# An attention block with softmax row sums: normalising the probabilities on GpSimd, and grouping the probability-value steps

## The chip, the cores and the metric

The kernel runs on one core of one Trainium2 chip. The metric is the device time of one execution in microseconds. Engines are named as in the profile: PE is TensorE, DVE is VectorE, ACT is ScalarE, POOL is GpSimd, SP is SyncE, whose queue issues the DMAs.

## The reference

```python
mod = (_silu(L0_c) @ L0_wmod).reshape(L0_c.shape[0], 6, 1, -1)
sa, ca, ga, sb, cb, gb = (mod[:, 0], mod[:, 1], mod[:, 2], mod[:, 3], mod[:, 4], mod[:, 5])
...
h = _layernorm(x, axis=-1) * (1 + ca) + sa
x = x + ga * _L0_attn_ref(h, ...)
h = _layernorm(x, axis=-1) * (1 + cb) + sb
x = x + gb * _L0_ffn_ref(h, ...)        # 160 experts, 8 chosen per token, and a shared one
```

and in the attention part, with 4 batches of 512 tokens of 128 values, 16 heads of 64:

```python
scores = jnp.einsum('bhqd,bhkd->bhqk', q, k) * scale + bias      # bias by relative position
attn = jax.nn.softmax(scores, axis=-1)
a = jnp.einsum('bhqk,bhkd->bhqd', attn, v)
return a.transpose(0, 2, 1, 3).reshape(B, S, N_HEAD * HEAD_DIM) @ o_w.T
```

Everything is float32. Where a plain float32 product would be too slow, values are split in a high and a low part, and three products are summed (`PASSES`).

## The kernel before

The attention stage takes the first half of the span, the experts the second; the change touches the first alone. Its unit of work is a pair of heads: 8 pairs per batch, 32 in all. A pair has 8 units (`UNITS`), each the 128 queries of one of its two heads against all 512 keys. The code is written once as `pair(b, n)` on each engine, and each engine's `pair` lists its own steps in an order written by hand; semaphores alone tie the engines together. Pairs 0 and 1 stand ahead of a loop over three batches whose body is pairs 2 to 9 (8 and 9 are the next batch's 0 and 1), and the last batch's pairs 2 to 7 stand behind it. So the turn of a batch, with the loop's jump, lies between pair 9 and the next pair 2.

A unit goes this way. `scores` (L426, two matmuls, L434 and L436) fills one of two PSUM banks. `add_bias` (L1016, one instruction of L1028 and a read of its accumulator) adds the bias on VectorE, writes `s_sb`, one of two buffers, and yields `nmax`, the negated maximum. `exponential` (L742) on ScalarE writes `prob`, one of four buffers, and the row sum into `rsum`. `transpose_probs` (L447) turns the unit over in four 128x128 transposes into one of two PSUM banks, and `copy_probs` takes it to `PT`: even units on ScalarE, odd ones on VectorE (both by the helper of L229). When all eight are there, `attend` (L455) multiplies `PT` with the values in four blocks of keys, kb 0 to 3, two heads each, and accumulates in PSUM.

The probabilities are not normalised before that product. Instead `invert_sums` (L1040) inverts the pair's eight row sums at once, `widen_sums` (L903) on GpSimd repeats them to 128x512 in `rinv_wide`, `spread_sums` (L474) transposes that on TensorE (L479) through one of the two banks that the probabilities' transposes use, `copy_sums` (L757, L762) on ScalarE brings it to `r_sb`, and VectorE's `normalise` (L1044) multiplies the attended values with it on the way to `oT`. A table, `transpose_users` (L58), counts who uses the two banks. `project_out` (L482) follows two pairs later.

Projections for later pairs run between: `project_qk` (L397) for pair n + 2 at the end of pair n; `qk_high` (ScalarE, L740) and `qk_low` (VectorE, L1013) split its result in the middle of pair n + 1; then SyncE's `stack_pair` (L280) rearranges it by DMAs, two after `qk_high` and six after `qk_low`. `project_v` (L413) for pair n + 1 stands in pair n and is copied by `copy_v` (ScalarE, L768). The next batch's input, `hcur`, is loaded when `project_v` of pair 7 is done (L320), and `project_qk` of pair 8 waits for it. At the turn of a batch VectorE also runs `gate_y`, `update_x` (L1069) and `new_statistics` (L1061).

## Time and profile before

| | |
|---|---|
| median of three runs | 1040.71 us (1038.21 to 1040.87) |
| profiled execution | 1039.4 us, span 1037.6 us |
| busy, of the span | PE 94%, DVE 74%, ACT 67%, POOL 2% |
| mean granted TensorE clock | 0.988 |

The attention stage ends near 543 us of the span. A busy share tells how long an engine had instructions in work, not what bounds: that is read from the chain of waits, followed back from the last instruction. In the rows further below, a timeline row is start, duration, engine, line and operation, and what stands in brackets is how long the engine was idle before it and who released it.

### The profile page before, as it was taken

To read this page: it belongs to the slowest core of one execution; us is meant where nothing else is said; L and a number is where in the kernel's file an instruction comes from. 1 tells how busy PE (TensorE), PEld (TensorE's weight loads), DVE (VectorE), ACT (ScalarE), POOL (GpSimd) and SP (SyncE) were. 2 spreads that over 40 slices of the span, in tenths; PEclk is the share of its full clock that TensorE was granted. 3 is DMA by queue.
4 is the path that set the end of the run, shared out by engine and by line. 5 is a ranking of instruction groups with operands and counts; after the bars stand their busy time and mean duration, and the time that the engine had idled before them with its cause. 6 is when DMAs were issued, how large, how long until landed. Compare 5 with 4: busy or idle time off the path is not lost.

```text
span 1037.6 us, 16983 instructions
## 1 busy us (share of the span) xinstructions
PE 974.3 (94%) x4720; PEld 704.8 (68%) x4720; DVE 770.4 (74%) x1356; ACT 696.6 (67%) x1200; POOL 20.0 (2%) x36
## 2 busy tenths in 40 slices
PE   4899999999999999999978699999999999999997
PEld 2565656566666666666643487888888888888886
DVE  5766656566566665666655488999999999999997
ACT  4556656566665666666645567777777777777775
POOL 0000000000000000000000000000000000000000
PEclk9999999999999999999998899999999999999999
DMA  7874353443543534534500499999999999999992
GB/s 211 270 200 107 80 140 82 103 108 80 137 106 78 122 88 115 122 82 102 122 21 1 135 219 221 220 218 220 219 217 222 219 219 219 220 218 221 219 219 66
DMA packets 71106, 160.49 MB, mean 155 GB/s; under 512 B 10272, under 2 KB 36192, under 8 KB 60944
## 3 DMA queue, kind: packets, MB, share of 16 engines
q1 hardware_dynamic: 71056, 159.97, 68.3%
q8 instruction: 14, 0.23, 0.1%
q14 instruction: 36, 0.29, 0.1%
HBM read 105.60 MB, written 2.42 MB: 104 GB/s over the span
## 4 chain that ended last, share of the span: by engine, by line
PE 86%; ACT 4%; DMA 3%; DVE 3%; issue 2%; SPq 2%; DVEq 0%; ACTq 0%
PE ps L658 41%; PE ps L466 11%; PE ps L451 9%; PE ps L434 5%; PE ps L436 5%; PE ps L408 4%; PE ps L419 2%; PE ps L487 2%; PE ps L479 2%; ACT r_sb L762 2%; DMA k_low<-qk 1%; DMA hcur<-hT 1%; SPq L298 1%; DMA comb_rows<-strips 1%; PE ps L576 1%
## 5 line engine op out<-in xcount | busy, mean ns | idle before, releaser
L747 ACT ACTIVATE prob<-s_sb,nmax 128x512 f32<-128x512 f32 x256 | 183.6, 718 | 114.1 <-DVE nmax L1028 113.5
L658 PE MATMUL ps<-hT,wT 128*128 128x512 f32 x960 | 244.6, 391 | 0.3 <-DVE wT L1191 0.3
L1210 DVE TENSOR_TENSOR PT<-v_sb,strips 128x1024 f32<-128x1024 f32 x160 | 195.8, 1224 | 43.2 <-ACT v_sb L879 29.7
L658 PEld LDWEIGHTS ps<-hT,wT 128*128 128x128 f32 x960 | 180.8, 189 | 39.1 <-ACT strips L854 1.1
L658 PE MATMUL ps<-stack,wT 128*128 128x512 f32 x640 | 198.3, 392 | 9.0 <-DVE wT L1197 9.0
L879 ACT ACTIVATE v_sb<-ps 128x1024 f32<-128x1024 f32 x160 | 164.4, 1028 | 60.1 <-PE ps L658 59.8
L229 DVE COPY PT<-ps 128x512 f32<-128x512 f32 x128 | 88.3, 690 | 145.2 <-PE ps L451 145.0
L1197 DVE TENSOR_TENSOR wT<-PT,stack 128x1024 fp32r<-128x1024 f32 x160 | 194.8, 1218 | 0.0
L871 ACT CAST stack<-PT 128x1024 fp32r<-128x1024 f32 x160 | 166.7, 1042 | 9.0 <-DVE PT L1210 9.0
L1028 DVE CUSTOM_DVE_ANT_0 s_sb<-ps,strips 128x512 f32<-128x512 f32 x256 | 166.8, 688 | 6.6 <-PE ps L436 6.5
L451 PE MATMUL ps<-ident,prob 128*128 128x128 f32 x1024 | 140.9, 275 | 12.0 <-ACT r_sb L762 8.7
L451 PEld LDWEIGHTS ps<-ident,prob 128*128 128x128 f32 x1024 | 117.4, 141 | 42.7 <-issue 18.5
L658 PEld LDWEIGHTS ps<-stack,wT 128*128 128x128 f32 x640 | 120.3, 189 | 36.0 <-DVE wT L1197 11.1
L466 PE MATMUL ps<-PT,v_sb 128*64 128x512 f32 x512 | 123.8, 603 | 4.3 <-ACT PT L229 2.8
L434 PE MATMUL ps<-stack 128*128 128x512 f32 x256 | 113.5, 443 | 3.1 <-DMA k_low<-qk 3.1
L658 PE MATMUL ps<-wT 128*128 128x512 f32 x320 | 99.1, 391 | 0.0
L229 ACT COPY PT<-ps 128x512 f32<-128x512 f32 x128 | 73.6, 575 | 10.8 <-PE ps L451 6.9
L466 PEld LDWEIGHTS ps<-PT,v_sb 128*64 128x64 f32 x512 | 33.1, 136 | 64.0 <-issue 50.7
L658 PEld LDWEIGHTS ps<-wT 128*128 128x128 f32 x320 | 60.3, 189 | 12.7
L408 PE MATMUL ps<-hcur,wT 128*128 128x512 f32 x192 | 52.8, 412 | 10.5 <-DMA hcur<-hT 4.8
L866 ACT CAST wT<-strips 128x256 fp32r<-128x256 f32 x80 | 32.4, 406 | 38.9 <-DMA strips<-in_L_ffn_w_down 38.8
L434 PEld LDWEIGHTS ps<-stack 128*128 128x128 f32 x256 | 49.1, 192 | 11.4 <-DVE nmax L1028 2.0
(108 smaller groups left out, 758.4 us busy)
## 6 DMA issues: line engine op xcount, KB each, us to landing
strips<-comb_rows SPq DMA_DIRECT2D x158, 512.0 KB, 13.2
stack<-qk SPq DMA_DIRECT2D x128, 256.0 KB, 3.8
k_low<-qk SPq DMA_DIRECT2D x64, 128.0 KB, 3.7
hT<-qk SPq DMA_DIRECT2D x64, 128.0 KB, 3.7
strips<-bias_rows SPq DMA_DIRECT2D x3, 1792.0 KB, 10.2
strips<-in_L_ffn_w_gate SPq DMA_DIRECT2D x80, 64.0 KB, 11.6
strips<-in_L_ffn_w_down SPq DMA_DIRECT2D x80, 64.0 KB, 13.6
strips<-bias_rows SPq DMA_DIRECT2D x2, 896.0 KB, 5.2
```

The source lines that it names most:

```text
L229: return copy(dst[:, :, qt * P:(qt + 1) * P], ps[:, BANK_T + number % 2, :].rearrange("p (k s) -> p k s", s=P))
L408: last = nc.tensor.matmul(ps[:, BANK_PROJ + part, :], wT[:, a, part * H * HD + hp * P:part * H * HD + (hp + 1) * P], hcur[:, m, :], start= ...
L434: nc.tensor.matmul(ps[:, BANK_S + g % 2, :], stack[:, par, head, 0, qt * P:(qt + 1) * P], stack[:, par, head, 1, :], start=True, stop=False)
L451: last = nc.tensor.transpose(ps[:, bank, kb * P:(kb + 1) * P], prob[:, u % 4, kb * P:(kb + 1) * P], ident[:, :])
L466: last = nc.tensor.matmul(ps[head * HD:(head + 1) * HD, BANK_O, :], v_sb[:, (n // 2) % 2, kb, (n % 2) * P + head * HD:(n % 2) * P + (head ...
L658: last = nc.tensor.matmul(ps[:, bank + c, :], weights(a), rows(m, c), start=start and k == 0, stop=stop and k == 2, skip_group_check=True)
L747: nc.scalar.activation(prob[:, u % 4, :], s_sb[:, u % 2, :], ACT.Exp, bias=nmax[:, u % 4:u % 4 + 1], scale=-1.0, accum_out=rsum[:, n % 2, ...
L871: nc.scalar.copy(h_high[:, k % 4, :], weighted[:, k % 4, :]).then_inc(s_hh, 1)
L879: nc.scalar.activation(silu[:, k % 2, :], ps[:, BANK_G + 2 * half:BANK_G + 2 * half + 2, :].rearrange("p c s -> p (c s)"), ACT.Silu).then_ ...
L1028: nc.vector.tensor_tensor_reduce(out=s_sb[:, u % 2, :], in0=ps[:, BANK_S + u % 2, :], in1=backwards, scale=-1.0, scalar=3.0e38, op0=ALU.ad ...
L1197: nc.vector.tensor_tensor(h_low[:, k % 4, :], weighted[:, k % 4, :], h_high[:, k % 4, :].bitcast(F32), ALU.subtract).then_inc(s_hl, 1)
L1210: nc.vector.tensor_tensor(weighted[:, k % 4, :], silu[:, k % 2, :], cb[:, r, half * HALF:(half + 1) * HALF], ALU.mult).then_inc(s_mul, 1)
```

## The change

GpSimd multiplies each unit's probabilities by its inverted row sum, in place, before they are transposed (`normalise`, eight 128x512 multiplies per pair). For that, `invert_sums` inverts two sums at a time, four times per pair. `rinv_wide`, `spread_sums`, `copy_sums`, `r_sb` and the table of bank users go, and VectorE's multiply to `oT` becomes a copy, `copy_o`. `prob` has eight buffers, one per unit, and `add_bias` writes straight into it, so `s_sb` goes; `add_bias` of a unit now waits until the same unit of the pair before has been transposed.

The hand-written orders change too. TensorE runs all four `attend` blocks together after scores 5, `project_v` ahead of scores 4, and each unit's transposes two places later in the order than before. ScalarE's `qk_high` and VectorE's `qk_low` now stand at the end of pair n, for pair n + 2. In the diff, lines of `...` mark what is left out.

```diff
-        s_sb = sb("s_sb", [P, 2, S])
-        prob = sb("prob", [P, 4, S])
-        r_sb = sb("r_sb", [P, S])
+        prob = sb("prob", [P, UNITS, S])
         oT = sb("oT", [P, 2, S])
         yT = sb("yT", [P, S])
-        nmax = sb("nmax", [P, 4])
-        rsum = sb("rsum", [P, 2, UNITS])
-        rinv = sb("rinv", [P, 2, UNITS])
-        rinv_wide = sb("rinv_wide", [P, QT, P])
+        nmax = sb("nmax", [P, UNITS])
+        rsum = sb("rsum", [P, UNITS])
+        rinv = sb("rinv", [P, UNITS])
...
+        def copied(b, g):
+            return (s_ca if g % 2 == 0 else s_cd), b * (G // 2) + (g // 2 + 1)
...
+            def transpose_probs(b, n, u):
+                g = UNITS * n + u
+                pe.wait_ge(s_prob, b * G + (g + 1))
+                if g >= 2:
+                    pe.wait_ge(*copied(b, g - 2))
...
+                    last = nc.tensor.transpose(ps[:, BANK_T + u % 2, kb * P:(kb + 1) * P],
+                                               prob[:, u, kb * P:(kb + 1) * P], ident[:, :])
...
-            def spread_sums(b, n, final):
-                pe.wait_ge(s_wide, b * HPAIRS + (n + 1))
-                bank = bank_for(b, ("R", n, 0), final)
-                for qt in range(QT):
-                    last = nc.tensor.transpose(ps[:, bank, qt * P:(qt + 1) * P], rinv_wide[:, qt, :], ident[:, :])
-                last.then_inc(s_t, 1)
...
                 if n >= 1:
-                    transpose_probs(b, n - 1, 6, final)
-                    transpose_probs(b, n - 1, 7, final)
+                    transpose_probs(b, n - 1, 4)
+                    transpose_probs(b, n - 1, 5)
                 scores(b, n, 2)
                 scores(b, n, 3)
-                if n >= 1:
-                    attend(b, n - 1, 0, final)
-                    attend(b, n - 1, 1, final)
-                    spread_sums(b, n - 1, final)
-                transpose_probs(b, n, 0, final)
-                transpose_probs(b, n, 1, final)
-                scores(b, n, 4)
-                scores(b, n, 5)
-                if n >= 1:
-                    attend(b, n - 1, 2, final)
-                    attend(b, n - 1, 3, final)
                 if n == 0:
                     project_v(b, 0)
                 if not (final and n >= HPAIRS - 1):
                     project_v(b, n + 1)
-                transpose_probs(b, n, 2, final)
-                transpose_probs(b, n, 3, final)
+                if n >= 1:
+                    transpose_probs(b, n - 1, 6)
+                    transpose_probs(b, n - 1, 7)
+                scores(b, n, 4)
+                scores(b, n, 5)
+                if n >= 1:
+                    for kb in range(QT):
+                        attend(b, n - 1, kb)
+                transpose_probs(b, n, 0)
+                transpose_probs(b, n, 1)
                 scores(b, n, 6)
                 scores(b, n, 7)
...
                 if n == HPAIRS + 1:
                     transpose_y(b)
                 if not (final and n >= HPAIRS - 2):
                     project_qk(b, n + 2)
-                transpose_probs(b, n, 4, final)
-                transpose_probs(b, n, 5, final)
+                transpose_probs(b, n, 2)
+                transpose_probs(b, n, 3)
...
+                nc.scalar.activation(prob[:, u, :], prob[:, u, :], ACT.Exp, bias=nmax[:, u:u + 1],
+                                     scale=-1.0, accum_out=rsum[:, u:u + 1]).then_inc(s_exp, 1)
...
             def pair(b, n, final=False):
+                exponential(b, n, 0)
+                exponential(b, n, 1)
+                if n == 0:
+                    qk_high(b, 1)
                 if n >= 1:
                     copy_probs(b, n - 1, 4)
-                exponential(b, n, 0)
-                exponential(b, n, 1)
+                exponential(b, n, 2)
+                exponential(b, n, 3)
+                if n == 0:
+                    copy_v(b, 0)
+                if not (final and n >= HPAIRS - 1):
+                    copy_v(b, n + 1)
                 if n >= 1:
                     copy_probs(b, n - 1, 6)
-                if not (final and n >= HPAIRS - 1):
-                    qk_high(b, n + 1)
-                exponential(b, n, 2)
-                if n >= 1:
-                    copy_sums(b, n - 1, final)
-                exponential(b, n, 3)
-                copy_probs(b, n, 0)
                 exponential(b, n, 4)
                 exponential(b, n, 5)
                 if n == 0:
-                    copy_v(b, 0)
                     first_high(2)
                     first_high(3)
-                if not (final and n >= HPAIRS - 1):
-                    copy_v(b, n + 1)
-                copy_probs(b, n, 2)
+                copy_probs(b, n, 0)
                 exponential(b, n, 6)
                 exponential(b, n, 7)
+                if not (final and n >= HPAIRS - 2):
+                    qk_high(b, n + 2)
+                copy_probs(b, n, 2)
...
-            def widen_sums(b, n):
-                pool.wait_ge(s_rinv, b * HPAIRS + (n + 1))
-                if n >= 1:
-                    number, _, _ = tables[False][1]["R", n - 1, 0]
-                    pool.wait_ge(s_t, b * NU + (number + 1))
-                pool.sem_inc(apart, 1)
-                nc.gpsimd.tensor_copy(rinv_wide[:, :, :].rearrange("p q (h d) -> p q h d", h=2),
-                                      rinv[:, n % 2, :].rearrange("p (h q o) -> p q h o", h=2, o=1).broadcast_to(
-                                          [P, QT, 2, HD])).then_inc(s_wide, 1)
-            widen_sums(0, 0)
-            with pool.Fori(0, B - 1) as b:
-                for n in range(1, HPAIRS + 1):
-                    widen_sums(b, n)
-            for n in range(1, HPAIRS):
-                widen_sums(B - 1, n)
+            def normalise(b, n, u):
+                if u % 2 == 0:
+                    pool.wait_ge(s_rinv, b * (G // 2) + (UNITS * n + u) // 2 + 1)
+                    pool.sem_inc(apart, 1)
+                nc.gpsimd.tensor_scalar(prob[:, u, :], prob[:, u, :], rinv[:, u:u + 1], None,
+                                        ALU.mult).then_inc(s_prob, 1)
+            with pool.Fori(0, B) as b:
+                for n in range(HPAIRS):
+                    for u in range(UNITS):
+                        normalise(b, n, u)
...
+                if g == UNITS - 1:
+                    dve.wait_ge(grp_used, 2)
+                if n >= 1:
+                    dve.wait_ge(s_t, b * G + (g - UNITS + 1))
...
-                nc.vector.tensor_tensor_reduce(out=s_sb[:, u % 2, :], in0=ps[:, BANK_S + u % 2, :],
+                nc.vector.tensor_tensor_reduce(out=prob[:, u, :], in0=ps[:, BANK_S + u % 2, :],
...
-            def invert_sums(b, n):
-                dve.wait_ge(s_exp, b * G + UNITS * (n + 1))
-                nc.vector.reciprocal(rinv[:, n % 2, :], rsum[:, n % 2, :]).then_inc(s_rinv, 1)
-            def normalise(b, n, final):
+                copy_unit(nc.vector.tensor_copy, n, u).then_inc(s_cd, 1)
+            def invert_sums(b, n, u):
+                g = UNITS * n + u
+                dve.wait_ge(s_exp, b * G + (g + 2))
+                if n >= 1:
+                    dve.wait_ge(s_prob, b * G + (g - UNITS + 2))
+                nc.vector.reciprocal(rinv[:, u:u + 2], rsum[:, u:u + 2]).then_inc(s_rinv, 1)
+            def copy_o(b, n):
                 dve.wait_ge(s_pv, b * HPAIRS + (n + 1))
-                dve.wait_ge(*copied(b, ("R", n, 0), final))
                 if n >= 2:
                     dve.wait_ge(s_ymm, b * HPAIRS + (n - 1))
-                nc.vector.tensor_tensor(oT[:, n % 2, :], ps[:, BANK_O, :], r_sb[:, :], ALU.mult).then_inc(s_o, 1)
+                nc.vector.tensor_copy(oT[:, n % 2, :], ps[:, BANK_O, :]).then_inc(s_o, 1)
...
             def pair(b, n, final=False):
+                add_bias(b, n, 0)
+                add_bias(b, n, 1)
+                if n == 0:
+                    first_low(1)
+                    qk_low(b, 1)
                 if n >= 1:
                     copy_probs(b, n - 1, 5)
-                add_bias(b, n, 0)
-                add_bias(b, n, 1)
-                if n >= 1:
-                    invert_sums(b, n - 1)
-                    copy_probs(b, n - 1, 7)
-                if n == 0:
-                    first_low(1)
+                invert_sums(b, n, 0)
                 add_bias(b, n, 2)
                 add_bias(b, n, 3)
-                if not (final and n >= HPAIRS - 1):
-                    qk_low(b, n + 1)
-                if n == HPAIRS + 1:
-                    gate_y(b)
                 if n == 0:
                     modulate(2)
                     modulate(3)
-                copy_probs(b, n, 1)
+                if n >= 1:
+                    copy_probs(b, n - 1, 7)
+                invert_sums(b, n, 2)
                 add_bias(b, n, 4)
                 add_bias(b, n, 5)
+                if n == HPAIRS + 1:
+                    gate_y(b)
                 if n == 0:
                     qkv_low(3)
                     qkv_low(4)
                     qkv_low(5)
-                if n >= 1:
-                    normalise(b, n - 1, final)
-                copy_probs(b, n, 3)
+                copy_probs(b, n, 1)
+                invert_sums(b, n, 4)
                 add_bias(b, n, 6)
                 add_bias(b, n, 7)
                 if n == 0:
                     first_low(2)
                     first_low(3)
+                if n >= 1:
+                    copy_o(b, n - 1)
+                copy_probs(b, n, 3)
+                invert_sums(b, n, 6)
+                if not (final and n >= HPAIRS - 2):
+                    qk_low(b, n + 2)
```

TensorE in the middle of a batch, from scores 5 of a pair on; L434 and L436 are `scores`, L466 `attend`, L451 the transposes, L419 `project_v`. Before:

```order
L434 MATMUL ps<-stack 128x512 [waits biased]
L436 MATMUL ps<-hT,stack 128x512
L466 MATMUL ps<-PT,v_sb 64x512 x4
L416 REGISTER_ALU
L419 MATMUL ps<-wT,hcur 128x256 [waits qk_low]
L419 MATMUL ps<-wT,hcur 128x256 x5
L444 REGISTER_ALU [waits exped]
L451 MATMUL ps<-ident,prob 128x128 [waits copied_by_act]
L451 MATMUL ps<-ident,prob 128x128 x3
L444 REGISTER_ALU [waits exped]
L451 MATMUL ps<-ident,prob 128x128 [waits copied_by_dve]
L451 MATMUL ps<-ident,prob 128x128 x3
```

(These are blocks 2 and 3; blocks 0 and 1 stand behind scores 3, with L479 behind them.) With the change, where L433 is `attend`, L420 the transposes, L409 and L411 the scores:

```order
L409 MATMUL ps<-stack 128x512 [waits biased]
L411 MATMUL ps<-k_low,stack 128x512
L428 REGISTER_ALU
L433 MATMUL ps<-PT,v_sb 64x512 [waits v_copied,o_copied,copied_by_dve,copied_by_act]
L433 MATMUL ps<-PT,v_sb 64x512 x7
L420 MATMUL ps<-ident,prob 128x128 [waits copied_by_act,normalised]
L420 MATMUL ps<-ident,prob 128x128 x3
L420 MATMUL ps<-ident,prob 128x128 [waits copied_by_dve,normalised]
L420 MATMUL ps<-ident,prob 128x128 x3
L408 REGISTER_ALU
L409 MATMUL ps<-stack 128x512 [waits biased]
L411 MATMUL ps<-k_low,stack 128x512
```

All eight matmuls of the four blocks stand in a row (x1 and x7), wait for both engines' copies, and only behind them come transposes 0 and 1, which wait for `normalised` and no longer for `exped`.

VectorE, from the last `add_bias` of a pair into the next pair. Before (L1028 `add_bias`, L229 `copy_probs`, L1042 `invert_sums`):

```order
L1028 ISA s_sb,nmax<-ps,strips 128x512 [waits scores,exped]
L1028 ISA nmax 128x1
L1035 REGISTER_ALU
L229 COPY PT<-ps 128x4x128 [waits transposed]
L1020 REGISTER_ALU
L1028 ISA s_sb,nmax<-ps,strips 128x512 [waits scores,exped]
L1028 ISA nmax 128x1
L1020 REGISTER_ALU
L1028 ISA s_sb,nmax<-ps,strips 128x512 [waits scores,exped]
L1028 ISA nmax 128x1
L1042 RECIPROCAL rinv<-rsum 128x8 [waits exped]
```

With the change (L971 `add_bias`, L204 `copy_probs`, L988 `invert_sums`, L954 `qk_low`):

```order
L204 COPY PT<-ps 128x4x128 [waits transposed]
L988 RECIPROCAL rinv<-rsum 128x2 [waits normalised,exped]
L953 REGISTER_ALU
L954 TENSOR_TENSOR qk<-ps,qk 128x1024 [waits qk_high]
L961 REGISTER_ALU
L971 ISA prob,nmax<-ps,strips 128x512 [waits scores,transposed,ld_strips4]
L971 ISA nmax 128x1
L961 REGISTER_ALU
L971 ISA prob,nmax<-ps,strips 128x512 [waits scores,transposed]
L971 ISA nmax 128x1
L204 COPY PT<-ps 128x4x128 [waits transposed]
L988 RECIPROCAL rinv<-rsum 128x2 [waits normalised,exped]
```

`qk_low` has moved from the middle of a pair to the place between its last reciprocal and the next pair's first `add_bias`, and a reciprocal that waits for ScalarE's exponentials now stands behind every second `add_bias`.

ScalarE, exponentials 6 and 7 and what follows, before (L747 `exponential`, L229 `copy_probs`, L740 `qk_high`, L762 `copy_sums`):

```order
L747 ACTIVATE prob,rsum<-s_sb,nmax 128x512 [waits transposed,biased] x2
L229 COPY PT<-ps 128x4x128 [waits transposed]
L740 CAST qk<-ps 128x1024 [waits stack_odd,qk_projected]
L747 ACTIVATE prob,rsum<-s_sb,nmax 128x512 [waits transposed,biased]
L762 COPY r_sb<-ps 128x512 [waits o_normed,transposed]
L747 ACTIVATE prob,rsum<-s_sb,nmax 128x512 [waits transposed,biased]
```

and with the change (L701 `exponential`, L697 `qk_high`, L204 `copy_probs`, L714 `copy_v`):

```order
L700 REGISTER_ALU
L701 ACTIVATE prob,rsum<-prob,nmax 128x512 [waits biased]
L694 REGISTER_ALU
L697 CAST qk<-ps 128x1024 [waits stack_odd,qk_projected]
L204 COPY PT<-ps 128x4x128 [waits transposed]
...
L700 REGISTER_ALU
L701 ACTIVATE prob,rsum<-prob,nmax 128x512 [waits biased]
L700 REGISTER_ALU
L701 ACTIVATE prob,rsum<-prob,nmax 128x512 [waits biased]
L714 COPY v_sb<-ps 128x512 [waits v_projected]
L204 COPY PT<-ps 128x4x128 [waits transposed]
```

`qk_high` stands right behind exponential 7, and copy 6 (the last row) behind `copy_v` and exponential 3 of the next pair.

## Rows read from the trace of the kernel before

**Rows 1.** The page, busy time by engine, and the chain that ended last by engine.

```profile
PE 974.3 (94%) x4720; PEld 704.8 (68%) x4720; DVE 770.4 (74%) x1356; ACT 696.6 (67%) x1200; POOL 20.0 (2%) x36
...
PE 86%; ACT 4%; DMA 3%; DVE 3%; issue 2%; SPq 2%; DVEq 0%; ACTq 0%
```

**Rows 2.** Chain of waits over one pair: start us, duration us, what.

```profile
338.36 1.94 PE ps L466 x8
...
340.99 0.59 ACT r_sb L762
...
341.63 0.66 PE ps L451 x4
...
343.22 1.87 PE ps L466 x8
...
345.99 0.87 PE ps L451 x8
...
353.70 0.61 PE ps L466
```

**Rows 3.** List of waits: us in total, times, longest.

```profile
ACT prob L747 <- DVE nmax L1028: 113.5, 96, 3.2
```

**Rows 4.** Timelines of PE, DVE and ACT of the same pair, from transposes 2 and 3 on.

```profile
345.83 1.04 PE L451 MATMUL ps<-ident,prob 128*128 128x128 f32 x8
...
346.90 0.69 DVE L229 COPY PT<-ps 128x512 f32<-128x512 f32 x1 [0.92 <-PE ps L451]
347.55 0.69 DVE L1028 CUSTOM_DVE_ANT_0 s_sb<-ps,strips 128x512 f32<-128x512 f32 x1
...
348.29 0.72 ACT L747 ACTIVATE prob<-s_sb,nmax 128x512 f32<-128x512 f32 x1 [1.18 <-DVE nmax L1028]
348.92 0.19 ACT L747 ACTIVATION_READ_ACCUMULATOR prob<-s_sb,nmax 128x1 f32 x1
349.01 0.71 ACT L747 ACTIVATE prob<-s_sb,nmax 128x512 f32<-128x512 f32 x1
...
349.71 0.56 ACT L229 COPY PT<-ps 128x512 f32<-128x512 f32 x1
```

**Rows 5.** Groups by line, the reciprocal (busy us, mean ns).

```profile
L1042 DVE RECIPROCAL rinv<-rsum 128x8 f32<-128x8 f32 x32 | 6.3, 198 | 0.4 <-ACT prob L747 0.4
```

**Rows 6.** Timelines of ACT and DVE, `qk_high` and `qk_low` of early pairs.

```profile
48.77 1.01 ACT L740 CAST qk<-ps 128x1024 fp32r<-128x1024 f32 x1
...
49.81 1.22 DVE L1013 TENSOR_TENSOR qk<-ps,qk 128x1024 fp32r<-128x1024 f32 x1 [0.47 <-ACT qk L740]
...
35.48 1.22 DVE L1013 TENSOR_TENSOR qk<-ps,qk 128x1024 fp32r<-128x1024 f32 x1
36.61 1.52 DVE L967 TENSOR_SCALAR PT<-ps,modT 128x512 f32<-128x512 f32 x2
```

**Rows 7.** Timeline of ACT, `copy_v` and the copy of unit 2 behind it.

```profile
346.03 0.59 ACT L768 COPY v_sb<-ps 128x512 f32<-128x512 f32 x1 [0.81 <-PE ps L419]
346.51 0.59 ACT L229 COPY PT<-ps 128x512 f32<-128x512 f32 x1
```

**Rows 8.** Timeline of POOL, `widen_sums` on both sides of a batch turn.

```profile
303.12 0.62 POOL L910 COPY rinv_wide<-rinv 128x512 f32<-128x512 f32 x1 [14.64 <-PE ps L451]
...
337.03 0.62 POOL L910 COPY rinv_wide<-rinv 128x512 f32<-128x512 f32 x1 [14.80 <-PE ps L451]
```

**Rows 9.** List of waits, TensorE for the next batch.

```profile
PE ps L408 <- DMA hcur<-hT: 4.8, 3, 2.1
```

**Rows 10.** Timeline of DVE at the turn of a batch.

```profile
314.76 0.68 DVE L1069 TENSOR_TENSOR x_all<-x_all,ps 128x512 f32 x1
...
319.34 0.69 DVE L229 COPY PT<-ps 128x512 f32<-128x512 f32 x1 [2.73 <-PE ps L451]
```

**Rows 11.** Timeline of all engines, GpSimd beside `add_bias`.

```profile
47.74 0.61 POOL L910 COPY rinv_wide<-rinv 128x512 f32<-128x512 f32 x1 [47.29 <-DVE rinv L1042]
...
48.04 0.68 DVE L1028 CUSTOM_DVE_ANT_0 s_sb<-ps,strips 128x512 f32<-128x512 f32 x1
```

89 lines of the change are left out of this document (20 added, 69 removed).

## The prediction

> **What bounds the kernel now.** I read the page first. TensorE is busy 94% of the span, VectorE 74%, ScalarE 67%, GpSimd 2%, and the chain that ended last is 86% TensorE [rows 1]. So in the attention stage, which the change touches, TensorE's own list of work sets the pace, and the question is what the change takes off that list and what it puts in the way of it.
>
> The chain of waits over one pair in mid-batch shows the list [rows 2]. From one first probability-value block to the next is 353.70 - 338.36 = 15.34 us. All of it is TensorE's work except one place: after the first two blocks (1.94) come the four transposes of `rinv_wide`, then ScalarE's copy to `r_sb` (from 340.99, 0.59), and only then, at 341.63, the transposes that need that bank. Between 338.36 + 1.94 = 340.30 and 341.63 TensorE gets one unit of useful transposing done, 0.44 us (half of the 0.87 that two take further on). So spreading the sums costs 341.63 - 340.30 - 0.44 = 0.89, and the unit behind the wait takes 0.66 instead of 0.44, another 0.22: about 1.1 us per pair. TensorE's list without it is about 15.34 - 1.1 = 14.2 us.
>
> The list of waits shows that the other two engines follow TensorE with room to spare: ScalarE stood idle 113.5 us in 96 places for VectorE's `nmax` [rows 3]. That room is what the change spends.
>
> **Removed.** Per pair: the transposes of L479, the copy of L762, GpSimd's widening, and the multiply in `normalise` (a plain copy takes its place, at the same length within a few hundredths, off the path). Worth 1.1 us x 32 = 35 us if TensorE stays the bound. I claim it does not.
>
> **The new ring.** Three things meet in the new order. `qk_high` and `qk_low` stand at the end of a pair, right behind exponentials 6 and 7 on ScalarE and ahead of the next pair's first `add_bias` on VectorE. `invert_sums` stands on VectorE between `add_bias` 1 and 2 and waits for exponential 1, so VectorE can't work ahead of ScalarE. And all four blocks stand together and wait for ScalarE's copy 6, which is behind exponentials 2 and 3. Nothing feeds VectorE with scores during the four blocks except 4 and 5, which are through early. So each block of four waits for work that begins only after the block of four before it. I walk once round, start to start:
>
> 1. Four blocks: two take 1.87 [rows 2], four 3.74.
> 2. Transposes 0 and 1, from their start to VectorE's copy 1, as transposes 2 and 3 to copy 3: 346.90 - 345.83 = 1.07 [rows 4].
> 3. That copy to the next instruction: 0.65 [rows 4]. `invert_sums`: 0.20, from the 198 ns of today's reciprocal [rows 5]; two columns instead of eight will hardly be shorter.
> 4. `add_bias` 6 to exponential 6: 348.29 - 347.55 = 0.74. Exponential 6 to 7: 0.72. Exponential 7 to `qk_high`: 0.70, by the copy that follows one today [rows 4].
> 5. `qk_high` to `qk_low`: 49.81 - 48.77 = 1.04. `qk_low` to the next VectorE instruction: 36.61 - 35.48 = 1.13 [rows 6].
> 6. Next pair, `add_bias` 0 to exponential 0: 0.74, to exponential 1: 0.72. Exponential 1 to the end of its accumulator read: 348.92 + 0.19 - 348.29 = 0.82 [rows 4], and 0.04 to hand over: 0.86. `invert_sums`: 0.20.
> 7. `add_bias` 2 to exponential 2: 0.74, to 3: 0.72, to `copy_v`: 0.70 [rows 4]. `copy_v` to the copy behind it, copy 6: 346.51 - 346.03 = 0.48 [rows 7].
> 8. Copy 6 to the blocks: 341.63 - 340.99 = 0.64, as today's ScalarE copy releases TensorE [rows 2].
>
> Sum: 3.74 + 1.07 + 0.85 + 2.16 + 2.17 + 2.52 + 2.64 + 0.64 = 15.8 us. That is more than the 15.34 of today and far more than TensorE's 14.2. TensorE will wait about 1.6 us per pair: most of it ahead of the four blocks, some ahead of scores 2, whose bank waits for `add_bias` 0 behind `qk_low`. Today the same instructions hang on no ring: the conversions stand mid-pair, ahead of a stretch in which VectorE waits for transposes anyway.
>
> **GpSimd.** Eight 128x512 multiplies per pair are new, and no row shows one. The lower bound is its copy of the same size, 0.62 [rows 8]; for the upper end I take four times that, 2.5, since a row of this arithmetic is missing altogether. It is nearest to the copy in shape and engine, so I take 0.6 to 1.2. The multiplies lie beside the ring: 6 and 7 start about with `qk_low`, and transposes 6 come only after its 1.13, `add_bias` 0, scores 2 and 3 and `project_v`, over 3.5 us later; for the other units it is longer. They decide from 15.8 / 8 = 2.0 us each.
> The Trainium skill (GPSIMD Engine Reference, 3.1 Elementwise) speaks against the move: it puts an elementwise loop on this engine at 1.8 to 2.6 cycles per element and calls it the wrong engine for such work. By those figures I estimate 0.77 to 1.1 us each; the sum would be the same, as both are under 2.0.
>
> **The sum against the profiled execution (1039.4 us).**
> - Pairs 3 to 30, 28 of them: 28 x (15.8 - 15.34) = +12.9.
> - `hcur`: `project_v` now stands ahead of scores 4 and 5, and SyncE reaches the load behind the six `qk_low` transfers of one pair, which are free to start when pair 6 of the batch begins; so it leaves about 5 us earlier (an estimate) and lands before `project_qk` asks. Today TensorE waits 4.8 us for it in three places [rows 9]: -4.8.
> - Turn of a batch: from `update_x` to the first VectorE instruction of the next pair are 319.34 - 314.76 = 4.58 us, loop jump included [rows 10]. They now lie between `qk_low` and `add_bias` 0, on the ring. Today two pairs with a turn take 337.03 - 303.12 = 33.91 against 30.68, so it costs 3.2 [rows 8]. Two turns: +1.4 each. The third has no jump back; I estimate +1.5 for it, from the 4.58 - 2.73 = 1.85 that are `update_x` and statistics. +4.3.
> - The first three pairs: the stack of pair 2 is there earlier, since its `qk_low` comes a third of a pair sooner; VectorE's setup work now lies on the ring. Together +1.5, an estimate, -2 to +5.
> - The last pair: no `project_qk` and no next scores cover the multiplies, and transposes 4 wait for copy 2 behind exponentials 6 and 7 and a multiply. +2.7, an estimate of three hand-overs from the steps above.
>
> 12.9 - 4.8 + 4.3 + 1.5 + 2.7 = +16.6: 1056.0. The profiled run lay 1.3 under the median of 1040.7, so **1057 us**. An error of 0.1 us in the ring is 2.8 us of time.
>
> **Rivals.**
> *A: the ring does not close, and TensorE stays the bound (the other side).* It decides where the ring is shorter than about 15.1, 0.7 under my walk. For it: ScalarE's many idle places. Against: each step of the walk is a measured distance. Price: 28 x (14.2 - 15.34) = -32, with -4.8 and perhaps +3: about 1007. Chance 0.08.
> *B: GpSimd is the bound.* At 2.2 us each a pair takes 17.6 and more: 28 x 2.3 + 4 = +68, about 1109. Nothing in the trace speaks for it but the missing row. Chance 0.05.
> *C: GpSimd and VectorE hold each other up.* Multiplies 0, 1 and 4, 5 run beside `add_bias` 2, 3 and 6, 7, which are on the ring. If two of those four waited out a multiply, the ring would grow by 2 x 0.6: 28 x 1.2 = +34, about 1091. Against it: `add_bias` at 48.04 runs beside GpSimd's copy of 47.74 and takes 0.68, its usual length [rows 11]. Chance 0.06.
> The Trainium skill (Perfetto Trace Analysis, Optimizing Scalar/DVE Operations) warns of this: the two share an SBUF read port, so moving work between them might not help. Its page SBUF — State Buffer (Who interferes with whom) narrows that to VectorE instructions with two SBUF inputs or in a two-port mode, and the trace agrees in the one overlap there is, with 0.68.
> That the change does not do what it says has no room: the listings show the removed rows gone.
>
> **How the numbers follow.** Forecast 0.81; A 0.08; B 0.05; C 0.06. The forecast's own range is the ring at 15.5 to 16.2 with the estimated ends: 1045 to 1070. A is left out below and B above, with most of C; 1045 to 1075 holds about 0.8. A measurement of this kernel tells about 0.3%, 3 us, from no change. Faster by more: A, 0.08. Within: the low end of the forecast (ring 15.1 to 15.3), 0.04. Slower: 0.88.
>
> **What would show it.** Right: a distance of 15.5 to 16.2 between first probability-value blocks in mid-batch; TensorE's largest waits on L466's successor for ScalarE's copy to `PT`, about 1.1 us each, and on scores 2 for `nmax`; ScalarE and VectorE in the chain with far more than 4% and 3%; no wait for `hcur`; GpSimd's rows at 0.6 to 1.2 us. Wrong: a distance under 15.1 with the chain still TensorE (A); transposes that wait for `prob` from GpSimd with its rows back to back (B); `add_bias` rows, or distances, longer than 0.62 beside GpSimd's (C); or a ring of the right length at other instructions, by which the walk would be right by luck.

## The result and the profile after

The changed kernel takes **1055.64 us** (median of four runs, 1054.25 to 1056.91) against 1040.79 for the kernel before in the same runs. The recorded ratio is 1.0148, 95% interval [1.0127, 1.0169] (the two medians alone give 1.0143). It is slower by 15 us; 1057 was predicted. The profiled execution took 1055.38 us with a span of 1053.6, 16.0 us longer than the 1037.6 before.

The page, busy time by engine, the chain that ended last by engine, and the new instruction's group (busy us, mean ns):

```profile
PE 961.7 (91%) x4592; PEld 695.9 (66%) x4592; DVE 777.6 (74%) x1452; ACT 679.7 (65%) x1168; POOL 398.2 (38%) x260
...
PE 67%; issue 11%; ACT 9%; DVE 6%; DMA 4%; SPq 2%; DVEq 1%; POOL 1%; ACTq 0%; POOLq 0%
...
L854 POOL TENSOR_SCALAR prob<-prob,rinv 128x512 f32<-128x512 f32 x256 | 398.0, 1570 | 150.7 <-DVE rinv L988 149.0
```

Against [rows 1] TensorE has 128 instructions fewer and 12.6 us less to do, and yet the span grew. Its share of the chain fell from 86% to 67%. ScalarE rose from 4% to 9%, VectorE from 3% to 6%, and 11% is "issue", time in which the profile shows no wait: partly the hand-overs between engines, partly time inside running instructions (in mid-batch 0.9 us of a round's lie inside `qk_low`).

In the list of waits (us in total, times, longest) TensorE's wait for ScalarE's copy to `PT` has grown tenfold, while that for the load of `hcur` [rows 9] is gone. Before:

```profile
PE ps L466 <- ACT PT L229: 2.8, 4, 1.0
```

and after:

```profile
PEld ps L420 <- POOL prob L854: 33.4, 45, 2.0
...
PE ps L433 <- ACT PT L204: 27.2, 27, 1.2
...
PE ps L409 <- DVE nmax L971: 11.2, 8, 3.7
```

The row of `PEld` is no time by itself: it counts waits of the weight load, under which the matmuls mostly went on (they themselves wait for GpSimd 1.9 us in 3 places). Of the 11.2 us of the last row 7.4 are two turns of a batch, one of them shown below.

Timelines of PE, DVE and ACT for one round in mid-batch, from one block of four to the next. The rows are in the order of the predicted walk:

```profile
350.31 3.65 PE L433 MATMUL ps<-PT,v_sb 128*64 128x512 f32 x16 [1.03 <-ACT PT L204]
353.90 1.09 PE L420 MATMUL ps<-ident,prob 128*128 128x128 f32 x8
...
355.03 0.69 DVE L204 COPY PT<-ps 128x512 f32<-128x512 f32 x1 [4.09 <-PE ps L420]
355.64 0.15 DVE L988 RECIPROCAL rinv<-rsum 128x2 f32<-128x2 f32 x1
355.71 0.67 DVE L971 CUSTOM_DVE_ANT_0 prob<-ps,strips 128x512 f32<-128x512 f32 x1
...
357.85 0.99 ACT L697 CAST qk<-ps 128x1024 fp32r<-128x1024 f32 x1
...
358.90 1.21 DVE L954 TENSOR_TENSOR qk<-ps,qk 128x1024 fp32r<-128x1024 f32 x1
360.02 0.68 DVE L971 CUSTOM_DVE_ANT_0 prob<-ps,strips 128x512 f32<-128x512 f32 x1
...
362.58 0.69 DVE L971 CUSTOM_DVE_ANT_0 prob<-ps,strips 128x512 f32<-128x512 f32 x1
...
365.21 0.58 ACT L204 COPY PT<-ps 128x512 f32<-128x512 f32 x1
...
365.84 0.65 PE L433 MATMUL ps<-PT,v_sb 128*64 128x512 f32 x2 [1.04 <-ACT PT L204]
```

Round once takes 365.84 - 350.31 = **15.53 us**, where [rows 2] had 15.34. Piece by piece, measured against predicted: block to transposes 3.59 (3.74); to copy 1 1.13 (1.07); copy and invert 0.68 (0.85); `add_bias` 6 to `qk_high` 2.14 (2.16); through `qk_low` to `add_bias` 0 2.17 (2.17); to `add_bias` 2 2.56 (2.52); to copy 6 2.63 (2.64); to the block 0.63 (0.64). The ring closes, at the instructions named. TensorE, with some 14.5 us of work, waits 1.03 or 1.04 ahead of each block. One thing the walk did not have: `qk_low` is released by `qk_high`, which ends at 358.84, and could also start only behind copy 3 and invert 6 (358.82), since transposes 2 and 3 stand behind `project_qk`. Two arms of nearly one length meet there, and the profile's chain of waits goes by the second.

The turn of a batch, in the timelines of PE and DVE, and the granted clock (the fields are window, us, PE busy with its count, PEclk, DMA share, GB/s):

```profile
321.43 1.20 DVE L954 TENSOR_TENSOR qk<-ps,qk 128x1024 fp32r<-128x1024 f32 x1
322.55 0.68 DVE L1014 TENSOR_TENSOR x_all<-x_all,ps 128x512 f32 x1
...
328.23 0.69 DVE L971 CUSTOM_DVE_ANT_0 prob<-ps,strips 128x512 f32<-128x512 f32 x1 [3.83 <-issue]
...
323.29 1.12 PE L446 MATMUL ps<-oT,woT 128*128 128x512 f32 x2 [1.65 <-DVE x_all L1014]
...
328.98 0.79 PE L409 MATMUL ps<-stack 128*128 128x512 f32 x1 [3.70 <-DVE nmax L971]
```

```profile
324.00:329.00 5.00, 1.30 (x10) 0.99 0.96 229
329.00:332.00 3.00, 3.00 (x10) 0.50 0.02 6
```

TensorE stands still 5.35 us in two places. In the 5.00 us up to 329.00 it is busy for 1.30 at a granted clock of 0.99, and in the next 3.00 the granted clock is 0.50, its level of 1.2 GHz.

### The profile page after: what moved, and what is told of

Read it like the earlier page. It is cut to its first block, busy times and chain, and to the rows that moved or that the text cites. A ratio compares the mean times of both kernels' runs of the same rounds, so it can differ in the third digit from the quotient of the medians.

```text
span 1053.6 us, 16804 instructions
## 1 busy us (share of the span) xinstructions
PE 961.7 (91%) x4592; PEld 695.9 (66%) x4592; DVE 777.6 (74%) x1452; ACT 679.7 (65%) x1168; POOL 398.2 (38%) x260
## 4 chain that ended last, share of the span: by engine, by line
PE 67%; issue 11%; ACT 9%; DVE 6%; DMA 4%; SPq 2%; DVEq 1%; POOL 1%; ACTq 0%; POOLq 0%
PE ps L615 39%; PE ps L433 11%; PE ps L420 6%; ACT prob L701 5%; PE ps L383 4%; DVE prob L971 2%; PE ps L409 2%; PE ps L411 2%; DMA k_low<-qk 1%; DMA strips<-in_L_ffn_w_down 1%; ACT PT L204 1%; ACT v_sb L714 1%; DVE qk L954 1%; POOL prob L854 1%; SPq L313 1%
## 5 line engine op out<-in xcount | busy, mean ns | idle before, releaser
L854 POOL TENSOR_SCALAR prob<-prob,rinv 128x512 f32<-128x512 f32 x256 | 398.0, 1570 | 150.7 <-DVE rinv L988 149.0
L701 ACT ACTIVATE prob<-prob,nmax 128x512 f32<-128x512 f32 x256 | 183.0, 716 | 128.8 <-DVE nmax L971 126.7
L204 DVE COPY PT<-ps 128x512 f32<-128x512 f32 x128 | 88.3, 690 | 153.5 <-PE ps L420 152.6
L971 DVE CUSTOM_DVE_ANT_0 prob<-ps,strips 128x512 f32<-128x512 f32 x256 | 166.0, 685 | 17.2 <-issue 9.0
L420 PEld LDWEIGHTS ps<-ident,prob 128*128 128x128 f32 x1024 | 115.5, 141 | 60.1 <-POOL prob L854 33.4
L433 PE MATMUL ps<-PT,v_sb 128*64 128x512 f32 x512 | 118.6, 606 | 28.4 <-ACT PT L204 27.2
L420 PE MATMUL ps<-ident,prob 128*128 128x128 f32 x1024 | 138.6, 278 | 5.8 <-ACT PT L204 3.4
L409 PE MATMUL ps<-stack 128*128 128x512 f32 x256 | 117.3, 458 | 13.7 <-DVE nmax L971 11.2
L204 ACT COPY PT<-ps 128x512 f32<-128x512 f32 x128 | 74.0, 578 | 85.9 <-PE ps L420 85.9
L433 PEld LDWEIGHTS ps<-PT,v_sb 128*64 128x64 f32 x512 | 35.0, 138 | 97.4 <-issue 58.0
L409 PEld LDWEIGHTS ps<-stack 128*128 128x128 f32 x256 | 49.3, 192 | 33.7 <-DVE nmax L971 26.0
```

Source lines behind the costliest of these rows:

```text
L204: return copy(dst[:, :, qt * P:(qt + 1) * P], ps[:, BANK_T + u % 2, :].rearrange("p (k s) -> p k s", s=P))
L409: nc.tensor.matmul(ps[:, BANK_S + g % 2, :], stack[:, par, head, 0, qt * P:(qt + 1) * P], stack[:, par, head, 1, :], start=True, stop=False)
L420: last = nc.tensor.transpose(ps[:, BANK_T + u % 2, kb * P:(kb + 1) * P], prob[:, u, kb * P:(kb + 1) * P], ident[:, :])
L433: last = nc.tensor.matmul(ps[head * HD:(head + 1) * HD, BANK_O, :], v_sb[:, (n // 2) % 2, kb, (n % 2) * P + head * HD:(n % 2) * P + (head ...
L701: nc.scalar.activation(prob[:, u, :], prob[:, u, :], ACT.Exp, bias=nmax[:, u:u + 1], scale=-1.0, accum_out=rsum[:, u:u + 1]).then_inc(s_ex ...
L854: nc.gpsimd.tensor_scalar(prob[:, u, :], prob[:, u, :], rinv[:, u:u + 1], None, ALU.mult).then_inc(s_prob, 1)
```

## The experiments

Twelve kernels ran, each timed against the kernel before on the same chip. "Pair" is the distance between blocks of four, or halves of them, in mid-batch.

### Copy 6 ahead of `copy_v`

```diff
                 exponential(b, n, 3)
+                if n >= 1:
+                    copy_probs(b, n - 1, 6)
                 if n == 0:
                     copy_v(b, 0)
                 if not (final and n >= HPAIRS - 1):
                     copy_v(b, n + 1)
-                if n >= 1:
-                    copy_probs(b, n - 1, 6)
```

> ScalarE's copy 6 is moved ahead of copy_v. Theory (the ring of waits that closes over copy 6 and the block of four sets the period of 15.53 us, and TensorE's wait of 1.03 us ahead of each block is its visible end): the ring loses the 0.47 us that copy_v takes on ScalarE between exponential 3 and copy 6; a second ring, over invert 6 and qk_high, is close behind, so I take 15.1 to 15.3 us for a pair, the wait ahead of the block 0.6 to 0.8 us, and 28 x 0.25 to 0.4 = 7 to 11 us less than the change: 1045 to 1049 us. Rival (TensorE's own list with its wait-to-start gaps is the bound, and the wait ahead of the block would be filled by another): 15.5 us for a pair, 1054 to 1057 us.

Measured: 1043.16 us, ratio 1.0042 [1.0004, 1.0081]. Timeline of PE:

```profile
344.19 3.65 PE L433 MATMUL ps<-PT,v_sb 128*64 128x512 f32 x16 [0.54 <-ACT PT L204]
...
359.24 3.23 PE L433 MATMUL ps<-PT,v_sb 128*64 128x512 f32 x14 [0.55 <-ACT PT L204]
```

A pair is 15.05: 0.48 less, which is `copy_v`'s step, and the wait ahead of the block is shorter by the same. It is a little more than the 0.25 to 0.4 I expected, and 1043.16 lies under my 1045 to 1049: I had feared that a second ring would catch some of it. Both arms that meet at `qk_low` run on through copy 6, so this run can't tell them apart.

### Copy 6 between exponentials 2 and 3

```diff
                 exponential(b, n, 2)
+                if n >= 1:
+                    copy_probs(b, n - 1, 6)
                 exponential(b, n, 3)
...
-                if n >= 1:
-                    copy_probs(b, n - 1, 6)
```

> ScalarE's copy 6 goes between exponentials 2 and 3. Theory: the ring loses copy_v's 0.47 and an exponential's 0.72 on the way to the block of four, and then other rings and TensorE's own list of 14.2 us a pair are the bound: 14.5 to 14.9 us for a pair, 28 x 0.65 to 1.0 = 18 to 28 us less than the change, 1028 to 1038 us, faster than the kernel before. The wait ahead of the block falls below 0.3 us. Rival (TensorE's list is the bound as it runs): 1053 to 1057 us. Second rival (exponential 3 comes later, and with it invert 2 and its two multiplies, and the wait shifts to the transposes): 1050 to 1060 us, with waits for GpSimd ahead of transposes 2 and 3.

Measured: 1026.14 us, ratio 0.9883 [0.9851, 0.9915], faster than the kernel before. The chain of waits over one pair is now TensorE alone:

```profile
332.48 3.58 PE ps L433 x16
...
346.91 3.58 PE ps L433 x16
```

346.91 - 332.48 = 14.43 us. That is TensorE's own list; the prediction put it at 14.2. One move of a 0.58 us copy is worth 29 us.

### A multiply of 8 columns

```diff
-nc.gpsimd.tensor_scalar(prob[:, u, :], prob[:, u, :], rinv[:, u:u + 1], None,
+nc.gpsimd.tensor_scalar(prob[:, u, 0:8], prob[:, u, 0:8], rinv[:, u:u + 1], None,
```

> GpSimd multiplies only 8 of the 512 columns of each tile (the other columns stay unnormalised), so the multiply is nearly free and the order of all engines stays. Theory (the multiply's 1.57 us are covered by the step that the transposes were moved back, up to 2.0 us): the period stays at 15.4 to 15.55 us; what goes is GpSimd's 12 multiplies back to back in the first pairs, the waits for it at the turns and the end: 3 to 7 us less than the change, 1048 to 1053 us. Rival (the 3.1 us of two multiplies stand on the way to the block of four): 2 to 3 us less per pair, the bound is then TensorE's 14.2 us a pair, 1010 to 1020 us.

Measured: 1057.02 us, ratio 1.0163 [1.0133, 1.0193]. Group of GpSimd, timeline of PE, and the first pairs:

```profile
L854 POOL TENSOR_SCALAR prob<-prob,rinv 128x8 f32<-128x8 f32 x256 | 75.1, 305 | 472.5 <-DVE rinv L988 472.5
```

```profile
352.74 3.65 PE L433 MATMUL ps<-PT,v_sb 128*64 128x512 f32 x16 [1.02 <-ACT PT L204]
...
368.26 3.65 PE L433 MATMUL ps<-PT,v_sb 128*64 128x512 f32 x16 [1.03 <-ACT PT L204]
```

```profile
63.01 0.70 PE L409 MATMUL ps<-stack 128*128 128x512 f32 x1 [3.29 <-DMA k_low<-qk]
```

A pair stays 15.52, so in mid-batch the multiply costs nothing: shown. The total is not the 3 to 7 us less that I expected, but that doesn't mean that the waits for GpSimd were free everywhere. At the end they were not. In the change, TensorE there:

```profile
549.14 0.66 PE L420 MATMUL ps<-ident,prob 128*128 128x128 f32 x4 [0.89 <-POOL prob L854]
550.63 5.35 PE L433 MATMUL ps<-PT,v_sb 128*64 128x512 f32 x16 [0.83 <-issue]
```

The last block takes 5.35 us, at a granted clock of 0.52 from 550.60 to 554.00, where it takes 3.65 with 8 columns. The last three distances between first `project_out` matmuls are 39.8 us in the change and 36.2 with 8 columns: the full multiply costs 3.6 us at the end. Two other differences hide this in the total. The transfer to `k_low` was waited for 3.29 us where the change has 1.09, and the third `project_out` is 2.0 us later; that transfer is late by a different amount in each profile, so the first pairs can't be read to better than 2 us. And the experts, whose code is the same, take 500.2 us from the last `project_out` to the end instead of 496.8. Over all profiles of this case that stretch takes 496.6 to 504.1, and why is open; a comparison of totals carries it, one of pairs doesn't.

### A longer multiply

```diff
+nc.gpsimd.tensor_scalar(prob[:, u, 0:256], prob[:, u, 0:256], 1.0, None,
+                        ALU.mult).then_inc(s_once, 1)
+pool.wait_ge(s_once, b * G + (UNITS * n + u + 1))
+pool.sem_inc(apart, 1)
 nc.gpsimd.tensor_scalar(prob[:, u, :], prob[:, u, :], rinv[:, u:u + 1], None,
```

> Ahead of each multiply GpSimd multiplies the left half of the tile by 1.0, with a wait between the two, so that a tile takes it 0.8 + 0.1 + 1.57 = about 2.5 us. Theory: GpSimd decides from about 2.0 us a tile; 8 x 2.5 = 20 us for a pair, 4.5 us more than 15.53, 31 pairs: about 1180 to 1200 us, GpSimd busy or waiting for itself throughout the attention part. Rival (the multiply already stands on the path with its full length, two for each link): 2 x 0.9 = 1.8 us more per pair, 1105 to 1115 us.

Measured: 1212.63 us, ratio 1.1667 [1.1638, 1.1696]. Timeline of GpSimd:

```profile
337.20 0.85 POOL L855 TENSOR_SCALAR prob<-prob 128x256 f32<-128x256 f32 x1
338.25 1.56 POOL L859 TENSOR_SCALAR prob<-prob,rinv 128x512 f32<-128x512 f32 x1 [0.20 <-POOL prob L855]
339.78 0.85 POOL L855 TENSOR_SCALAR prob<-prob 128x256 f32<-128x256 f32 x1
```

339.78 - 337.20 = 2.58 us a tile, with no idle time but its own wait; 8 x 2.58 = 20.6, and blocks of four are 20.84 apart. The size was a little over what I expected (the hand-over 0.20 instead of 0.1); the kind is as the theory had it. With the run above this brackets the cover: at 1.57 us the multiply is free in mid-batch, at 2.58 GpSimd is the bound. Where between them it turns was not tried.

### Invert 0 behind `add_bias` 2

```diff
-                invert_sums(b, n, 0)
                 add_bias(b, n, 2)
+                invert_sums(b, n, 0)
                 add_bias(b, n, 3)
```

> VectorE's invert_sums of tiles 0 and 1 stands behind add_bias 2 instead of ahead of it, so that add_bias 2 no longer waits for exponential 1. Theory (the ring of 15.53 us also passes exponential 1 -> invert_sums 0 -> add_bias 2, as the chain of one pair shows, with VectorE idle there): that link falls from exponential 1's start + 0.84 + 0.28 to an order that VectorE reaches by itself; a walk of the remaining steps gives 15.0 to 15.2 us for a pair, TensorE's wait ahead of the block 0.5 us, 28 x 0.35 to 0.5 = 10 to 14 us less than the change: 1041 to 1046 us. Rival (the link is a tie with another and nothing is won): 15.4 to 15.5 us, 1052 to 1056 us.

Measured: 1036.22 us, ratio 0.9970 [0.9932, 1.0008]: not told apart from the kernel before, and 19 us under the change.

```profile
353.10 3.65 PE L433 MATMUL ps<-PT,v_sb 128*64 128x512 f32 x16 [0.35 <-ACT PT L204]
...
367.94 2.37 PE L433 MATMUL ps<-PT,v_sb 128*64 128x512 f32 x10 [0.35 <-ACT PT L204]
```

A pair is 14.84, and the time is 5 us under my range: the link was worth 0.69 us a pair, more than I had walked out. A reciprocal of 0.17 us, placed so that VectorE waits for ScalarE, cost the change more than its whole loss.

### The old order with the new multiply, and the same with 8 columns

```diff
-transpose_probs(b, n - 1, 4)
-transpose_probs(b, n - 1, 5)
+transpose_probs(b, n - 1, 6)
+transpose_probs(b, n - 1, 7)
...
-for kb in range(QT):
-    attend(b, n - 1, kb)
+attend(b, n - 1, 0)
+attend(b, n - 1, 1)
```

and so on in the three lists of a pair: the order is that of the kernel before, with each invert behind the exponentials it needs.

> One part alone: GpSimd's multiply and the sums inverted two at a time, but the order of all engines as in the kernel before (transposes 6 and 7 behind scores 1, the block of four split in two, transposes 0 and 1 behind scores 3, qk_high and qk_low in mid-pair). Theory (the move of the transposes by one step is what covers the multiply): the 3.1 us of two multiplies and the invert stand between exponentials and transposes, in a step of 3.8 us in which the exponentials alone leave some 1 to 2 us: 16.3 to 17.5 us for a pair, 1078 to 1110 us, with TensorE waiting for GpSimd ahead of most transposes. Rival (the new order costs, not the multiply): under 15.3 us for a pair, under 1045 us.

> As the run in the old order, but GpSimd multiplies 8 of the 512 columns (the others stay unnormalised): the old order without the transposed sums and with a nearly free multiply. Theory: four transposes and ScalarE's copy of the sums are gone and nothing new stands on the path but the inverts, 14.2 to 14.9 us for a pair, 1018 to 1035 us; the difference to the run with the full multiply, 1.8 us or more a pair, is what the multiply costs where it isn't covered. Rival (multiply covered in the old order too): same time as that run within 5 us.

Measured: 1082.70 us, ratio 1.0437 [1.0365, 1.0509], and 1016.87 us, ratio 0.9779 [0.9748, 0.9811]. Timeline of PE of the first:

```profile
395.76 0.66 PE L420 MATMUL ps<-ident,prob 128*128 128x128 f32 x4 [0.82 <-POOL prob L851]
397.27 1.94 PE L433 MATMUL ps<-PT,v_sb 128*64 128x512 f32 x8
...
413.82 1.94 PE L433 MATMUL ps<-PT,v_sb 128*64 128x512 f32 x8
```

and of the second:

```profile
339.75 1.94 PE L433 MATMUL ps<-PT,v_sb 128*64 128x512 f32 x8
...
353.99 1.94 PE L433 MATMUL ps<-PT,v_sb 128*64 128x512 f32 x8
```

Pairs of 16.55 and 14.24. In the old order the same multiply costs 2.3 us a pair, 66 us in all; in the order of the change it costs nothing in mid-batch. TensorE waits for GpSimd ahead of its transposes 62.9 us in 74 places in the first of these runs, and 1.9 in 3 in the change. The two orders differ in more than the transposes' place, so that their move by one step is what pays for GpSimd is read from these waits, not isolated. The 14.24 also confirms what the prediction computed for removing the spread sums.

### The block of four split again

```diff
-                    for kb in range(QT):
-                        attend(b, n - 1, kb)
+                    attend(b, n - 1, 0)
+                    attend(b, n - 1, 1)
...
                 scores(b, n, 7)
+                if n >= 1:
+                    attend(b, n - 1, 2)
+                    attend(b, n - 1, 3)
```

> The change with the block of four probability-value steps split again: two behind scores 5, two behind scores 7. Theory (all eight steps of a round of the ring lie on TensorE's and the two arms that tie; the second half of the block now stands ahead of project_qk and transposes 2 and 3, on the same ring): 15.4 to 15.65 us for a pair, 1052 to 1058 us, no change from the change's own 1055.6. Rival (the undivided block of 3.65 us is what holds up scores 6 and 7 and transposes 0 and 1, and with them the exponentials): 1.0 to 1.3 us less for a pair, TensorE without waits, 1020 to 1030 us.

Measured: 1063.01 us, ratio 1.0220 [1.0193, 1.0247].

```profile
355.31 1.94 PE L433 MATMUL ps<-PT,v_sb 128*64 128x512 f32 x8 [1.02 <-ACT PT L204]
...
371.19 1.94 PE L433 MATMUL ps<-PT,v_sb 128*64 128x512 f32 x8 [1.03 <-ACT PT L204]
```

A pair is 15.88, 0.35 worse, outside both expectations by size. The wait ahead of the first half stays. So the undivided block is not what costs. Where the 0.35 arises stands in the timeline of DVE:

```profile
363.57 0.69 DVE L204 COPY PT<-ps 128x512 f32<-128x512 f32 x1 [1.76 <-PE ps L420]
```

Copy 3 starts 363.57 - 355.31 = 8.26 us behind the block, and in the change 358.22 - 350.31 = 7.91. The second half stands ahead of `project_qk` and transposes 2 and 3, so it lengthens the arm through copy 3 and invert 6 by just what the pair grows. With that arm and the other within 0.1 us of each other, I should have expected it.

### The turn: `update_x` first, invert 0 too, and VectorE's loop written out

```diff
                 invert_sums(b, n, 6)
+                if n == HPAIRS + 1:
+                    update_x(b)
                 if not (final and n >= HPAIRS - 2):
                     qk_low(b, n + 2)
                 if n == HPAIRS + 1:
-                    update_x(b)
                     new_statistics(b)
```

> The best order so far (copy 6 between exponentials 2 and 3, 1026.1 us) with update_x ahead of VectorE's last qk_low in the pair that ends a batch. Theory (TensorE's 1.65 us ahead of the first project_out of a new batch are a wait for update_x, which stands behind qk_low's 1.1 us; but what stands behind that is the wait of 3.7 us for VectorE's first add_bias after its loop jump): the wait of 1.65 falls to about 0.5, the one of 3.7 grows by as much, since VectorE's work ahead of the jump is the same: 1025 to 1027 us. Rival (the wait is lost time by itself): 3 x 1.1 = 3 us less, 1022 to 1024 us.

Measured: 1020.97 us, ratio 0.9835 [0.9800, 0.9869]. The rival was right:

```profile
304.58 1.12 PE L446 MATMUL ps<-oT,woT 128*128 128x512 f32 x2 [0.52 <-DVE x_all L1014]
310.04 0.50 PE L409 MATMUL ps<-stack 128*128 128x512 f32 x1 [3.47 <-DVE nmax L971]
```

The first wait fell from 1.65 to 0.52 and the second did not take it over (3.72 in the run without this move). By their `project_out` distances the three turns are 1.1, 2.5 and 0.9 us shorter. The medians are 5.2 us apart, the profiled executions 2.7; 3 was the rival's figure, and the rest is not told from noise.

With invert 0 behind `add_bias` 2 as well:

> Copy 6 between exponentials 2 and 3, update_x ahead of qk_low at the turn (together 1021.0 us), and invert_sums 0 behind add_bias 2. Theory (with copy 6 moved, TensorE works without a wait at 14.42 us a pair, so a shorter ring is worth nothing in the middle; at most a little in the first pairs and behind a turn): 14.42 us for a pair, 1019 to 1022 us. Rival (TensorE still gives time back when the other engines run further ahead): 14.2 us for a pair, 1014 to 1016 us.

Measured: 1023.55 us, ratio 0.9873 [0.9805, 0.9941]: not told apart from the kernel without it. Where TensorE is the bound, the link that was worth 19 us is worth nothing.

Last, VectorE's loop over batches:

```diff
-            with dve.Fori(0, B - 1) as b:
+            for b in range(B - 1):
```

> As the 1021.0 us kernel, but VectorE's loop over the first three batches is written out (TensorE, ScalarE, GpSimd and SyncE keep theirs). Theory (TensorE's wait of 3.47 us at the start of each new batch is the 2.85 us that VectorE stands still at its loop jump, with the wait for that add_bias behind it): VectorE's idle time there goes, the wait falls to 0.7 to 1.2 us, 3 x 2.3 to 2.8 = 7 to 8 us less: 1013 to 1015 us. Rival (the longer program is fetched as slowly as the jump is, or ScalarE's jump is as long and stands behind it): the wait stays, 1019 to 1023 us.

> The kernel before with VectorE's loop over the first three batches written out, to tell how much of the 28 us by which the combined version is below the kernel before the loop is worth by itself. Theory (the turn is a cost of its own, that the kernel before has in part too: there TensorE waits 1.15 us for VectorE's copy behind the jump and 0.95 us for a copy ahead of the block): 3 x 1.2 to 2.1 = 4 to 6 us less than the kernel before, 1034 to 1037 us, and the order is worth the other 22 us. Rival (the jump is as dear there as in the combined version): 3 x 2.8 = 8 us less or more, 1030 to 1032 us.

Measured: **1012.81 us**, ratio 0.9727 [0.9702, 0.9752], with copy 6 and `update_x` moved; and 1032.12 us, ratio 0.9924 [0.9898, 0.9950], for the kernel before with nothing but the loop written out. Timeline of PE at the turn of the first:

```profile
301.39 0.50 PE L409 MATMUL ps<-stack 128*128 128x512 f32 x1 [0.52 <-DVE nmax L971]
```

The wait of 3.47 is 0.52, and with the half clock behind it gone too (0.50 from 312 to 315 us with the loop, 1.00 from 301 to 307 us without) the two turns that had a jump are 4.8 and 4.6 us shorter. In the kernel before they are only 2.1 and 2.6 shorter, together within the 4 to 6 that I expected. Its median fell by 7.9 all the same; of the rest, 1.5 us are in the pair with the first wait for `hcur` and 1.7 ahead of the first `project_out`, neither of them at a jump back, and the cause is open. So the two savings of 8 us are not shown to be the same 8. Of the 28 us below the kernel before, the change's idea in a better order gives 19 (1040.11 to 1020.97), and the loop the rest.

## Why the prediction was right, and where its terms were not

**The ring** is the mechanism, with four runs behind it: taking `copy_v` off it gives back exactly `copy_v`'s step, taking off the exponential too leaves TensorE alone, unhooking invert 0 gives 0.69, and putting half a block ahead of `project_qk` costs 0.35. Its size was off by 0.27 us: 15.8 predicted, 15.53 measured. Invert 4 on the way costs 0.07 (355.64 to 355.71), not the 0.20 that I took from the busy time in [rows 5], since the next instruction starts before it has ended; invert 0, which waits for ScalarE, costs 0.28. And four blocks take 3.59, not twice 1.87. The term "28 x (15.8 - 15.34) = +12.9" should have been 28 x 0.19 = +5.3. I had also put TensorE's waits at 1.6 us a pair, some of them ahead of scores 2; in mid-batch they are 1.03, all ahead of the block.

**GpSimd.** I estimated 0.6 to 1.2 us; the multiply takes 1.57, 2.5 times the copy in [rows 8]. The error cost nothing in mid-batch, because what I used it for was the point from which it decides, 2.0, and 12.6 us of multiplies a pair fit into 15.5. The nearest row was a copy, without arithmetic. The Trainium skill (GPSIMD Engine Reference, 3.1 Elementwise) gave me an estimate of 0.77 to 1.1, also too low. The Trainium skill (GPSIMD Engine Reference, its opening) also calls this engine the wrong choice for ordinary elementwise arithmetic. That holds for the length (VectorE's multiply of the same size in the kernel before took 0.69), not for the time of a pair here: with 8 columns it is the same 15.52.

**Rivals.** A fell: the ring is 0.4 above the 15.1 from which it decides, and two runs show what A would have been (1026 and, with the turn mended, 1021, where I had priced it at 1007). B fell at 1.57 us, and the longer multiply shows B itself. C fell: `add_bias` rows are 0.67 to 0.69 us long beside GpSimd's multiplies, as everywhere (the trace before had not one overlap with `add_bias` but three, at 48.04, 194.60 and 321.83, each 0.68 long), and the run in which GpSimd did a fifth of the work had the same pair. The rule of the Trainium skill on the shared port (Perfetto Trace Analysis, Optimizing Scalar/DVE Operations) does not bite for these operations.

**The turns** were under-sized: two at +1.4 and one at +1.5. Timelines of `project_out` around one turn, after; its distances in mid-batch are 15.52:

```profile
305.49 1.02 PE L446 MATMUL ps<-oT,woT 128*128 128x512 f32 x2
...
323.29 1.12 PE L446 MATMUL ps<-oT,woT 128*128 128x512 f32 x2 [1.65 <-DVE x_all L1014]
...
342.95 1.02 PE L446 MATMUL ps<-oT,woT 128*128 128x512 f32 x2
```

Two distances take 37.46 instead of 31.04, 6.4 over; with the next one, 6.9, against the 3.2 of [rows 8]. The three turns cost 4.6, 3.6 and 2.4 more than before, together 10.6 instead of 4.3. I had put `update_x` on the ring but not asked who waits for it: `project_out` of the new batch, and behind that the half clock.

**Start, end, `hcur`.** The third `project_out` and the last:

```profile
95.84 1.02 PE L446 MATMUL ps<-oT,woT 128*128 128x512 f32 x2
...
556.76 1.13 PE L446 MATMUL ps<-oT,woT 128*128 128x512 f32 x2 [0.79 <-DVE oT L994]
```

and in the kernel before:

```profile
94.06 1.02 PE L487 MATMUL ps<-oT,woT 128*128 128x512 f32 x2
...
540.07 1.12 PE L487 MATMUL ps<-oT,woT 128*128 128x512 f32 x2 [0.80 <-DVE oT L1049]
```

Start 95.84 - 94.06 = +1.8 (+1.5 predicted, and no better known than 2 us). `hcur`, by the three long distances before (one of 19.25, two of 16.90, where the others are 15.3): -7.1 (-4.8; behind the first wait, of 2.10 us, TensorE also ran at a granted clock of 0.57 from 141 to 144 us, which I had not counted). The last four distances are +5.9, of which 0.8 is the ring, so the end is +5.1 (+2.7); 3.6 of it is GpSimd's multiply with the half clock behind it, by the run with 8 columns. The rest of the program is 0.7 shorter. In all 5.3 + 10.6 - 7.1 + 1.8 + 5.1 - 0.7 = 15.0 of the 16.0; the last one stays unassigned. So the total was right within 1.4 us because a ring 7.6 us too dear and turns and an end 8.7 us too cheap offset each other, with `hcur` 2.3 us off the other way. The direction and the mechanism were earned; the last two digits were luck.

## What to carry to other kernels

When work is taken off the busiest engine and the order is changed with it, walk the chain from one landmark to the same landmark one iteration later, through every engine's list. If it is longer than that engine's list, what you removed is worth nothing, and the cure is not a faster instruction but taking instructions out of the way to the landmark: here one copy moved by two places gave 29 us. An operation on a slow side engine is judged by its deadline, not its length, and the deadline is made by the order; where no other work covers it, as at the end here, it costs again. At a loop's turn ask of each instruction you put there who waits for it.
